# A table look-up on TensorE as one fp32 matmul instead of three bf16 ones, in a fused tokenizer, attention and mixture-of-experts kernel

## The reference, cut to what matters

```python
y = _moe_mlp(hidden_states, sg_w, su_w, sd_w)
for i in range(E):                      # 16 experts
    gate_feature = hidden_states * pe[i] @ gate_w + gate_b
    gate_weight, gate_idx = jax.lax.top_k(gate_feature, K)       # the 96 largest of 192
    gate_weight = jax.nn.softmax(gate_weight, axis=-1)
    gathered = jnp.take_along_axis(hidden_states, gate_idx, axis=-1)
    y = y + _moe_mlp(gathered * gate_weight, eg_w[i], eu_w[i], ed_w[i])
```

## Time and profile before

| | us |
|---|---|
| runs | 2681.51, 2693.8, 2690.25 |
| their median | 2690.25 |
| the profiled execution | 2678.3 |
| its span, first to last instruction | 2676.5 |
| mean granted TensorE clock (1 is 2.4 GHz) | 0.851 |

### The profile page before, as it was taken

One profiled execution on the slowest core, in us unless ns is written; L12 is line 12 of the kernel. 1 busy time (PEld: TensorE's weight loads), 2 busy tenths in 40 slices (PEclk: granted clock), 3 DMA queues, 4 the chain that ended last, 5 costly groups with the idle time before them and its releaser, 6 DMA issues.

```text
span 2676.5 us, 49824 instructions
## 1 busy us (share of the span) xinstructions
PE 2215.7 (83%) x12378; PEld 1236.0 (46%) x12378; DVE 2488.0 (93%) x13377; ACT 1706.9 (64%) x3995; POOL 1729.7 (65%) x2202
## 2 busy tenths in 40 slices
PE   4478988888899878888988888889888888797876
PEld 3235545445454444454545544545445444353434
DVE  3699499999999999999999999999999999999970
ACT  2243677766767676767576756766766757665664
POOL 1123767766667677676676756766766667676666
PEclk8566899988988989898798979896988978877887
DMA  2211122322222222222222312221322222222210
GB/s 61 45 33 48 42 47 56 66 45 60 45 56 48 59 54 50 54 52 52 49 57 49 66 32 61 55 54 41 68 45 57 45 53 57 49 60 44 50 45 20
DMA packets 192518, 135.89 MB, mean 51 GB/s; under 512 B 107700, under 2 KB 180367, under 8 KB 192231
## 3 DMA queue, kind: packets, MB, share of 16 engines
q1 hardware_dynamic: 190756, 129.92, 21.9%
q0 software_dynamic: 928, 1.72, 0.2%
q10 hardware_dynamic: 546, 1.06, 0.1%
HBM read 102.68 MB, written 27.77 MB: 49 GB/s over the span
## 4 chain that ended last, share of the span: by engine, by line
DVE 84%; PE 7%; DMA 3%; issue 2%; ACT 2%; POOL 1%; SPq 1%; ACTq 0%; POOLq 0%; DVEq 0%
DVE idx L634 29%; DVE keys L636 28%; DVE vals L630 24%; DMA rows<-digit_d 1%; DMA digit_d<-dcode 1%; PE ps L1270 1%; DMA looked_s<-in_mask_in 1%; PE ps L1196 1%; DVE nmax L590 1%; SPq L471 1%; PE ps L1247 1%; DVE digits L611 1%; PE ps L1250 0%; PE ps L1207 0%; PE ps L1185 0%
## 5 line engine op out<-in xcount | busy, mean ns | idle before, releaser
L1034 POOL TENSOR_TENSOR picked<-looked_s,code 128x384 f32<-128x384 f32 (+1 forms) x912 | 819.8, 906 | 534.7 <-ACT looked_s L763 532.2
L634 DVE FIND_INDEX8 idx<-vals,keys 128x8 uint16<-128x192 f32 x2712 | 934.2, 345 | 0.0
L630 DVE MAX8 vals<-keys 128x8 f32<-128x192 f32 x2712 | 817.4, 340 | 52.0 <-ACT keys L722 52.0
L763 ACT ACTIVATE looked_s<-ps 128x384 f32<-128x384 f32 (+1 forms) x912 | 449.4, 493 | 652.1 <-PE ps L1196 649.4
L636 DVE MATCH_REPLACE8 keys<-vals,keys 128x192 f32<-128x192 f32 x2486 | 834.4, 336 | 0.0
L755 ACT ACTIVATE code<-ps 128x768 bf16<-128x768 f32 (+1 forms) x912 | 738.7, 810 | 93.3 <-PE ps L1185 83.1
L1196 PE MATMUL ps<-code,table 128*128 128x384 bf16 (+1 forms) x2736 | 669.9, 358 | 0.0
L1185 PE MATMUL ps<-rows,codew 17*128 17x384 bf16 (+1 forms) x1824 | 330.8, 359 | 280.7 <-ACT code L755 184.0
L1196 PEld LDWEIGHTS ps<-code,table 128*128 128x128 bf16 x2736 | 255.5, 106 | 321.0 <-issue 196.6
L1185 PEld LDWEIGHTS ps<-rows,codew 17*128 17x128 bf16 x1824 | 87.2, 92 | 631.1 <-ACT code L755 336.1
L1250 PE MATMUL ps<-xwt,wexp 96*96 96x128 f32 x1792 | 294.7, 316 | 38.5 <-ACT xwt L729 33.0
(11 more groups left out here) (149 smaller groups left out, 2300.5 us busy)
## 6 DMA issues: line engine op xcount, KB each, us to landing
wexp<-in_w_exp SPq DMA_DIRECT2D x58, 576.0 KB, 4.5
wdown<-in_w_down SPq DMA_DIRECT2D x58, 576.0 KB, 4.5
digit_d<-dcode SPq DMA_DIRECT2D x56, 384.0 KB, 2.6
rows<-digit_d SPq DMA_DIRECT2D x224, 96.0 KB
table<-parts SPq DMA_DIRECT2D x240, 9.0 KB
hr<-norm_d SPq DMA_DIRECT2D x112, 12.0 KB
patch<-in_patches SPq DMA_DIRECT2D x16, 108.0 KB, 4.9
tok_d<-h SPq DMA_DIRECT2D x16, 84.8 KB
```

The costliest lines, as they stand in the source:

```text
L630: nc.vector.max(vals[:, par, e, at], from_keys[:, e, :]).then_inc(chain, 1)
L634: found = nc.vector.max_index(idx[:, par, e, at], vals[:, par, e, at], from_keys[:, e, :])
L763: nc.scalar.activation(looked_s[:, o % 4, 0:w], ps[:, LOOK_B[o % 2], 0:w], ACT.Copy).then_inc(looked_out, 1)
L1034: nc.gpsimd.tensor_tensor(picked[:, o % PICKS, w], looked_s[:, o % 4, w], code[:, o % 4, 1, w], ALU.mult).then_inc(picked_ready, 1)
```

## The change

The table holds fp32 features as they are, and the look-up is one fp32 matmul. The stage, the split and the copies go; the table is loaded from `norm_d` in DRAM by 16 DMAs for each half instead of eight copies, with a quarter of the columns each. The first tile needs its 16 rows eight times over; for that, a new DRAM tensor `rest_d` is written once from `norm_d`, between two stores of image 0. The code is written as fp32, since both operands of the matmul are.

```diff
-TABLE = 16 * PER
+TABLE = 16 * PER * 2
...
-        table = sb("table", [128, OCT, 3, TILE], BF16)
+        table = sb("table", [128, OCT, TILE])
...
-        code = sb("code", [TILE, 4, 2, COLS], BF16)
+        code = sb("code", [TILE, 4, 2, COLS])
...
+                    if i == 0:
+                        first = norm_d[0:REST, :]
+                        sp.wait_ge(norm_out, 16)
+                        sp.dma_start(rest_d.rearrange("(e p) d -> e p d", e=PACK),
+                                     bass.AP(tensor=first.tensor, offset=first.offset,
+                                             ap=[[0, PACK]] + [list(x) for x in first.ap])).then_inc(rest_out, 16)
                     sp.wait_ge(misc_out, stage_out(i, "turn_h"))
                     sp.dma_start(normt_d[:, :, at], hst[:]).then_inc(normt_out, 16)
...
                 def build_table(t, part):
 
-                    sp.wait_ge(split, t + 1)
                     if t:
+                        sp.wait_ge(norm_out, 16 * last_image(t) + 16)
                         sp.wait_ge(looked, OCT * block_no(t, 0) - OCT // 2 * (1 - part))
-                    octs = slice(OCT // 2 * part, OCT // 2 * (part + 1))
-                    for j in range(PER):
-                        at = slice(HI * j, HI * (j + 1))
-                        sp.dma_start(table[at, octs, :, LO * j:LO * (j + 1)].rearrange("p o s l -> p (o s) l"),
-                                     parts[at, octs].rearrange("p o s l -> p (o s) l")).then_inc(table_in[part], 16)
+                        src = norm_d[start(t):start(t) + TILE, :]
+                    else:
+                        sp.wait_ge(rest_out, 16)
+                        src = rest_d
+                    src = src.rearrange("(q r j) (hi lo) -> r j hi q lo", q=QUADS, j=PER, lo=LO)
+                    for r in range(2 * part, 2 * part + 2):
+                        for j in range(PER):
+                            sp.dma_start(table[HI * j:HI * (j + 1), QUADS * r:QUADS * (r + 1), LO * j:LO * (j + 1)],
+                                         src[r, j]).then_inc(table_in[part], 16)
...
                     if g == 2 and t < TILES:
                         sp.wait_ge(gated, pairs_before(t + 1, 0))
                         load_gate(t + 1)
-                        sp.wait_ge(split, t + 1)
-                        load_tokens(t + 1)
...
-                    if (g == 3 and t < TILES or n == 0) and o in (1, 3, 5, 7):
-                        split_part(t + 1, o // 2)
...
-                    for s in range(3):
-                        ins = nc.tensor.matmul(ps[:, LOOK_B[o % 2], w], table[:, o, s, :], code[:, o % 4, 0, w],
-                                               start=(s == 0), stop=(s == 2))
+                    ins = nc.tensor.matmul(ps[:, LOOK_B[o % 2], w], table[:, o, :], code[:, o % 4, 0, w], start=True, stop=True)
```

More of the change, by code:

```diff
@@ L330, in build @@
         nt_rest = sb("nt_rest", [HALF, 2, REST])
-        hr = sb("hr", [HALF, OCT, LO])
-        rest = sb("rest", [HALF, OCT, LO])
-        parts = sb("parts", [HALF, OCT, 3, LO], BF16)
         resid = sb("resid", [TILE, D])
@@ L424, in store_image @@
                     sp.dma_start(norm_d[at, :], hs[:]).then_inc(norm_out, 16)
+                    if i == 0:
[4 more added lines that the diff above has]
+                                             ap=[[0, PACK]] + [list(x) for x in first.ap])).then_inc(rest_out, 16)
                     sp.wait_ge(misc_out, stage_out(i, "turn_h"))
                     sp.dma_start(normt_d[:, :, at], hst[:]).then_inc(normt_out, 16)
-                def load_tokens(t):
-                    sp.wait_ge(norm_out, 16 * last_image(t) + 16)
-                    for j in range(PER):
-                        if t == 0:
-                            for a in range(REST // PER):
-                                src = norm_d[PER * a + j, :].rearrange("(hi lo) -> hi lo", lo=LO)
-                                sp.dma_start(hr[HI * j:HI * (j + 1), :, :].rearrange("p (e a) l -> p a e l", e=PACK)[:, a],
-                                             bass.AP(tensor=src.tensor, offset=src.offset,
-                                                     ap=[list(src.ap[0]), [0, PACK], list(src.ap[1])])).then_inc(hr_in, 16)
-                        else:
-                            src = norm_d[start(t):start(t) + TILE, :].rearrange("(o j) (hi lo) -> j hi o lo", j=PER, lo=LO)[j]
-                            sp.dma_start(hr[HI * j:HI * (j + 1), :, :], src).then_inc(hr_in, 16)
                 def load_gate(t):
@@ L1073, in _ @@
                         pack()
-                for step in range(4):
-                    split_part(0, step)
                 square(0)
```

31 lines of the change are left out of this document (4 added, 27 removed).

## The result

The change made the kernel a little faster, not slower. The changed kernel takes 2666.8 us (median of 11 runs, 2659.9 to 2675.8), the kernel before 2681.4 (11 runs, 2669.9 to 2693.8): ratio 0.9942, interval 0.9922 to 0.9962. The forecast was 2708. Medians and ratios in this document are of fast executions; one execution of e13, 3200.3 us at a granted clock of 0.546, is left out of its median. The profiled execution has a span of 2660.1 us at a mean granted clock of 0.906, against 2676.5 at 0.851.

The account below looks back on a forecast made before the run. VectorE was taken to bound the middle by a hair, with the look-up chain close behind. Start +1, middle +13 and end +4 made +18 us, 2708 us against the 2690.25 median; its own range 2698 to 2725, the whole 2682 to 2760.

Parts of the forecast that it names:

- The end: After 2592 us, where VectorE is not waited for: 24 dearer look-ups add 4 us.
- SyncE's price: SyncE's queue: each new table load from DRAM holds it for 0.35 us, range 0.30 to 0.78.
- The -1.5 behind block 0: SyncE after block 0: 16 loads take 5.6 us instead of the copies' 7.06, so digits go out earlier.
- Rival C: SyncE: a table load costs as much queue time as a copy, 0.78 us; 2748 us in all, chance 0.07.
- The start: +1 forecast: Until VectorE's keys at 324 us: +8 from dearer look-ups, -7 from SyncE, together +1 us.
- The term +8: Start, 145 to 324 us: 52 dearer look-ups add 11 us, 8 after leaving out 23%.
- The middle: +13 forecast: Where VectorE sets the pace: 16 us of hold-up in 12 tight blocks, 5 in others, less 8 for the clock.
- the clock gave back 8: Middle: fewer TensorE gaps for rows mean fewer slow stretches, which takes 8 us off the added time.
- rival A: Middle: the cover swallows the added look-up time, so no change; 2687 to 2695, named 2691 us, chance 0.30.
- the room of 0.75 us: Middle, at 2073.57 us: keys start only 0.75 us ahead of VectorE, so a dearer look-up chain overtakes it.
- the +16: Middle, 12 tight blocks: VectorE is held up by 16 us after covers, waits for digits and room are subtracted.
- Rival B: Middle: the look-up chain becomes the bound, all look-ups on the path, no clock returned; +53, 2748 us, chance 0.20.

Follow-up runs that it names:

- e13: Kernel before, with three small VectorE instructions at a block's end in forms meant to avoid the port shared with GpSimd; 2672.9 us, ratio 0.9972.
- e4: Kernel before, with five bf16 matmuls in each look-up instead of three; 2670.9 us, ratio 0.9964.
- e2: Changed kernel, with three bf16 matmuls on a constant table and a bf16 code again, new DRAM loads kept; 2673.5 us, ratio 0.9968.
- e3: Kernel before, with four bf16 matmuls in each look-up instead of three; 2668.4 us, ratio 0.9956.
- e5: Changed kernel, with the first tile's table loaded by 8 wider DMAs instead of 32; 2661.8 us, ratio 0.9934.
- e8: Kernel before, with a fourth bf16 matmul in the look-ups of blocks 0 to 3 alone; 2682.4 us, ratio 1.0000.
- e11: Kernel before, with six bf16 matmuls in each look-up instead of three; 2681.2 us, ratio 0.9994.
- e12: Changed kernel, with the first table by 8 DMAs and three VectorE instructions at a block's end in other forms; 2656.5 us, ratio 0.9901.
- e6: Changed kernel, with GpSimd's split (on unread tiles) and SyncE's wait for it put back; 2674.7 us, ratio 0.9970.
- e7: e5 with 48 unread matmuls ahead of each wait for rows of blocks 1 and 2; 2662.5 us, ratio 0.9936.
- e9: Kernel before, with a fourth bf16 matmul in all look-ups from block 4 on; 2672.3 us, ratio 0.9979.

## Why the prediction was wrong

**What held.** The look-up costs 0.82 us at the fast clock, on two instructions. GpSimd's product takes 998 ns (forecast 996), with no effect on the time, and ScalarE's write costs nothing. VectorE does bound the middle, and the start counts in full. The end came out at +3 for +4 (the terms, 24 x 0.25 x 0.77, give 4.6; tails of 127.4 to 127.6 us before, 130.3 and 130.8 after), but that may be luck: with the kernel before's own look-ups e13 has 130.6, and with five bf16 matmuls e4 has 126.9.

**The base.** The forecast stood on 2690.25, the median of three runs; that of eleven is 2681.4. So 9 of the 41 us by which 2708 missed are of the base and not of the mechanism. The change itself was put at +18 us and measured at -14.6.

**SyncE's price, right in kind, 14% low.** I took 0.35 us an issue. The trace has 32 in 13.09, 0.41 each, because each issue of 0.37 is followed by a gap of 0.04 that I left out. The eight stage loads took 3.59 us with their gaps, not 3.1. Also, the first table load starts at 110.37 us, where before's first copy started at 109.29. So block 0's digits came 3.6 us earlier (128.92 to 125.30), not 5.6; the other executions have 129.80 and 130.97 before and 125.05 after. The -1.5 behind block 0 did not come: 16 loads hold the queue for 7.21 us there, where eight copies held it for 7.06. Rival C (0.78) is refuted.

**The start: +1 forecast, about -10 measured.** The term +8 for the dearer look-ups failed. The first nine steps of block 0, from ScalarE's end of taking the first look-up to its start on the ninth, took 20.7 us before (145.5 to 166.2) and 15.0 after (141.8 to 156.8). One window shows why, 145 to 167 us, before, and then after:

```profile
145.00:167.00 22.00, 21.43 (x92) 11.93 (x92) 22.00 (x121) 8.29 (x27) 8.62 (x18) 0.58 0.01 2
```

```profile
145.00:167.00 22.00, 19.09 (x116) 11.49 (x114) 22.00 (x122) 15.28 (x50) 11.09 (x19) 1.00 0.12 29
```

At a granted clock of 0.58 TensorE gets through 92 instructions, at 1.00 through 116. I priced each look-up at the clock of the old window (0.72) and asked what it adds, but never what it does to the clock. The nine steps take either 15.0 to 16.4 us (both of after, e2, e3, e4, e5, e8, e11, e12) or 19.3 to 20.8 (all of before, e6, e7, e9, e13), so it is a switch and not a slope. An added pass goes with the fast side (e3), and so does leaving out the split (e2). But the program alone does not set it: up to the ninth step e7 has the instructions of e5, and it fell on the other side. These are their nine steps, e5 and then e7, with 78 TensorE instructions each:

```profile
129.88:144.95 15.07, 14.56 (x78) 8.52 (x78) 15.07 (x83) 6.79 (x23) 6.71 (x13) 0.92 0.01 1
```

```profile
132.21:152.50 20.29, 20.06 (x78) 11.50 (x78) 20.29 (x113) 7.08 (x23) 6.76 (x13) 0.64 0.01 1
```

From the ninth step to block 5, before needs 146 to 158 us and after 147 and 153: no +8 there either. Nor is the switch the whole start. With slow steps and digits at 128.9 to 131.0 us (before, e9, e13) block 5 starts at 318 us on average; with fast steps alone (e2, e3, e4, e8, e11) at 315; with early digits alone (e6, 124.7) at 312.5; with both (after, 125.1 and 125.3) at 307.5. Single executions scatter by up to 11 us, so the shares are not shown.

**The middle: +13 forecast, -1 to -3 measured, and this is the step that failed.** In my sum 40 us of look-ups on 12 tight blocks became 31 on the path, then 16 of VectorE's idle time, and the clock gave back 8. The windows say that from 1553 to 2245 us, where the tight blocks are, the clock gave back nearly all. My price adds 256 x 0.21 = 54 us to TensorE there; its busy time is 603.9 us in the mean of the three executions before (598.6 to 607.0) and 609.4 in the two after (605.3 and 613.6), so some 6 us of it are left. In e3 the added stream is not even seen: 593.7 us. From 330 to 1553 us, at a clock of 0.90 before, about half came back (1047.6 us before, 1092.2 after, for some 86 added), and the other half stayed under VectorE's work.

Two things were wrong. First, the returned clock was put down as a small correction of a few gaps, though the earlier trace rows had 0.85 there, so that up to 15% of the stretch could come back; it was the largest cover in the profile. (The row pair 0.66 and 1.14 us also says that a slow look-up takes 1.7 times as long, and not twice, as I wrote under rival A.) Second, I read the room of 0.75 us, which was at block 45, as the state of the kernel. It was one draw: in the next two executions of before the keys of that block were 4.5 and 5.6 us ahead, while block 41's were 0.5 ahead and 4.6 late. In place of the +16, VectorE never waits after the start in either execution of the changed kernel, and its room grew: over the first blocks of the tiles behind block 5, the keys are at least 4.2 and 4.1 us ahead in its two executions, and 5.6 in e3, where the three of before have 0.24 and 0.50 us at least, and one wait. (The other versions with fp32, e5, e6, e7 and e12, have 1.8 to 4.6 us at least, and e2, three bf16 matmuls with the new loads, 4.2; so the loads take part in this.) ScalarE's waits for digits, which I forecast to fall from 90 us over the run, rose to 132.3 and 108.7.

The mean of the middle fell from 2230.1 us (three executions) to 2228.7 (two), or from 2231.9 if e8, whose middle is before's, is counted with the first.

**Rival A was the true mechanism,** by its sign (no VectorE idle time after the start) and by one of its two reasons: denser matmuls pay for themselves. The other reason, digits that go out on time and spare gaps, is not what raised the clock: in e2 TensorE waits less for rows (12.2 us from 1553 to 2250, against 18.2 to 21.8 in the three of before) at a clock of 0.848. I gave A 0.30 and 2691 us, and even that is 24 too high: 9 of it are the base, and its start stood at +1. Against it I had set only the room of 0.75 us. Rival B needs the clock at its end: in e11, with six passes, it begins to show.

**What stays open.** The means of the changed kernel's three stretches are 11 us down in the start, 1 in the middle and 3 up in the tail, together 10 less; the medians say 14.6, so some 5 us are not accounted for by the profiled executions. The medians of e3 and e9 are 12 and 9 us under before's, more than the stands and the waits at block 41 of single executions account for. Whether a denser TensorE also makes VectorE's stands rarer (kernels with three bf16 matmuls in the middle stand 12 to 24 us, the others 8 to 19) can't be told from so few executions.

## What to carry to other kernels

Where the granted clock is well under 1 and TensorE is not the bound, price a change of its work in busy time of the whole window, not by the instruction. In this kernel, at 0.85, a fourth pass of some 145 us cost 25 us of busy time and none of the kernel's; at 0.93 to 0.95 a sixth one cost 84 and 10. Room of under a microsecond, read once, is one draw; profile the unchanged kernel two or three times before a sum is built on it. And a bound engine that is "100% busy" may hold stands in which it does nothing: compare the durations of equal instructions.

## What the runs showed of the hardware

- More matmuls, higher clock: 0.851 (three bf16 in a look-up), 0.900 (four), 0.930 (five), 0.952 (six), 0.906 (one fp32). TensorE's busy time: 2215.7, 2240.9, 2327.1, 2411.1 and 2264.7 us.
- The same 78 TensorE instructions took 15.07 us at a granted clock of 0.92 (e5) and 20.29 at 0.64 (e7), in programs that are the same up to there.
- A VectorE TENSOR_SCALAR that else takes 0.25 us stood 2.55 us behind three GpSimd TENSOR_TENSORs in a row. All 333 such stands of 16 executions end within 0.06 us of the end of a GpSimd instruction; a TENSOR_REDUCE, MAX8 or MATCH_REPLACE8 showed none. This makes 8 to 24 us of 2660, and most of the scatter of the middle.
- A SyncE issue of 48 runs of 64 bytes from DRAM took 0.37 us and 0.04 to the next, one of 192 took 0.39 and 0.06 (eight in 3.59 us); a copy within SBUF of 288 short runs took 0.78 and 0.08 (16 in 13.68). The first table's eight issues in e5, of 192 runs each too, held SyncE for 4.22 us, 0.53 each.
